# Attention scores on two 64-row halves, two tiles at a time, in a two-layer attention kernel

## What is computed

```python
xn = group_norm(x, 32 groups) * w + b                      # x: (8, 512, 1024)
qkv = einsum('oc,bct->bot', qkv_w, xn) + qkv_b             # 8 heads x (q, k, v) x 64 rows
weight = softmax(einsum('bct,bcs->bts', q, k) / 8)         # 1024 x 1024 for each head
a = einsum('bts,bcs->bct', weight, v)
x = x + einsum('oc,bct->bot', proj_w, a) + proj_b
```

## Time and profile before

| | us |
|---|---|
| median of 3 runs | 4324.97 |
| lowest and highest | 4324.69 and 4325.98 |
| the profiled execution, its own time | 4325.91 |
| its span, first to last instruction | 4323.8 |
| PE busy | 4282.4 |
| DVE busy | 3287.5 |
| ACT busy | 2918.6 |
| POOL busy | 2435.6 |

### The profile page before, as it was taken

How to read it: one execution, slowest core, us unless ns; L and a number is a source line. 1 busy time by engine, 2 the same in 40 slices (tenths; PEclk the granted TensorE clock), 3 DMA queues, 4 the chain that set the end, 5 groups by cost and what they waited for, 6 DMA issues and landing times.

```text
span 4323.8 us, 89926 instructions
## 1 busy us (share of the span) xinstructions
PE 4282.4 (99%) x26692; PEld 3739.6 (86%) x26692; DVE 3287.5 (76%) x5479; ACT 2918.6 (67%) x5375; POOL 2435.6 (56%) x2332
## 2 busy tenths in 40 slices
PE   8999999999999999999999999999999999999999
PEld 6888888888888888888888888888888888888888
DVE  5777867788686886877867778687886877868787
ACT  4757847577575775757757577575775757767576
POOL 5655556465564655646566465564655646556464
PEclk9999999999999999999999999999999999999999
DMA  3232222322223222232222222222222222222222
GB/s 87 49 96 47 71 72 49 96 47 78 65 49 96 47 80 65 47 95 49 78 74 58 87 47 82 64 65 80 47 79 67 66 79 48 80 64 68 75 49 88
DMA packets 99645, 295.08 MB, mean 68 GB/s; under 512 B 15104, under 2 KB 15232, under 8 KB 99328
## 3 DMA queue, kind: packets, MB, share of 16 engines
q1 hardware_dynamic: 99328, 291.19, 25.0%
HBM read 123.36 MB, written 33.55 MB: 36 GB/s over the span
## 4 chain that ended last, share of the span: by engine, by line
PE 94%; DVE 3%; POOL 2%; issue 1%; ACT 1%; DMA 0%; DVEq 0%; SPq 0%; POOLq 0%
PE ps_t L780 21%; PE ps_g L734 15%; PE ps_o L792 11%; PE ps_o L793 11%; PE ps_s L771 11%; PE ps_s L769 11%; PE ps_s L734 7%; PE ps_t L734 4%; PE ps_o L734 2%; POOL x_raw L382 2%; DVE xn_lo L644 1%; DVE rstd_bits L630 0%; DVE seed L628 0%; ACT xn_hi L491 0%; DVE pt_lo L587 0%
## 5 line engine op out<-in xcount | busy, mean ns | idle before, releaser
L376 POOL TENSOR_SCALAR probs<-probs,row_rcp 128x1024 f32<-128x1024 f32 x1024 | 1154.2, 1127 | 1365.8 <-DVE row_rcp L582 1365.8
L578 DVE TENSOR_REDUCE row_min<-ps_s 128x1 f32<-128x1024 f32 x1024 | 1250.6, 1221 | 213.4 <-PE ps_s L771 198.6
L480 ACT CAST pt_hi<-ps_t 128x512 fp32r<-128x512 f32 x2048 | 1112.6, 590 | 432.2 <-PE ps_t L780 421.7
L587 DVE TENSOR_TENSOR pt_lo<-ps_t,pt_hi 128x512 fp32r<-128x512 f32 x2048 | 1309.5, 680 | 9.5 <-ACT pt_hi L480 5.0
L475 ACT ACTIVATE probs<-ps_s,row_min 128x1024 f32<-128x1024 f32 x1024 | 1150.9, 1124 | 211.0 <-DVE row_min L578 194.2
L780 PEld LDWEIGHTS ps_t<-const_sb,probs 128*128 128x128 f32 x8192 | 945.1, 140 | 180.1 <-DVE pt_lo L587 50.3
L780 PE MATMUL ps_t<-const_sb,probs 128*128 128x128 f32 x8192 | 1084.4, 274 | 3.6 <-DVE pt_lo L587 3.4
L792 PE MATMUL ps_o<-pt_hi,v_st 128*128 128x256 f32 x4096 | 1044.1, 288 | 0.0
L793 PE MATMUL ps_o<-pt_lo,v_st 128*128 128x256 f32 x4096 | 1015.0, 282 | 0.0
L771 PE MATMUL ps_s<-kl_st,q_st 128*128 128x512 f32 x2048 | 808.5, 395 | 0.0
L769 PE MATMUL ps_s<-kh_st,q_st 128*128 128x512 f32 x2048 | 806.9, 394 | 0.0
(11 more groups left out here) (117 smaller groups left out, 4959.8 us busy)
## 6 DMA issues: line engine op xcount, KB each, us to landing
wqk_raw<-in_wqk SPq DMA_DIRECT2D x130, 256.0 KB, 2.6
q_st<-kh_st SPq DMA_DIRECT2D x128, 256.0 KB, 2.9
q_st<-kl_st SPq DMA_DIRECT2D x128, 256.0 KB, 3.6
kh_st<-kh_st SPq DMA_DIRECT2D x128, 256.0 KB, 2.9
kl_st<-kl_st SPq DMA_DIRECT2D x128, 256.0 KB, 3.6
x_raw<-layer_out SPq DMA_DIRECT2D x36, 512.0 KB, 5.4
wv_raw<-in_wv SPq DMA_DIRECT2D x66, 256.0 KB, 4.4
x_raw<-in_x SPq DMA_DIRECT2D x32, 512.0 KB, 5.5
```

Of the source, the lines that this page charges most:

```text
L376: nc.gpsimd.tensor_scalar(probs[m % 2][:, :], probs[m % 2][:, :], row_rcp[:, m % 4:m % 4 + 1], 1.0, ALU.mult, ALU.mult).then_inc(probs_rea ...
L480: nc.scalar.copy(pt_hi[:, m // 2 % 2, 4 * half:4 * half + 4, (m % 2) * P:(m % 2 + 1) * P], ps_t[:, half, :].rearrange("p (b t) -> p b t", ...
L578: nc.vector.tensor_reduce(row_min[:, m % 4:m % 4 + 1], ps_s[:, m % 2, :], AX.X, ALU.min).then_inc(min_ready, 1)
L587: nc.vector.tensor_tensor(pt_lo[place], ps_t[:, half, :].rearrange("p (b t) -> p b t", b=4), f32(pt_hi[place]), ALU.subtract).then_inc(lo_ ...
```

## The change

It does five things.

1. Scores: `stack` now keeps the split result straight (`hi_st`, `lo_st`: q in rows 0 to 63, k in rows 64 to 127) and builds a swapped copy (`hi_sw`, `lo_sw`: q in rows 64 to 127, and the first half of k's columns in rows 0 to 63). `scores` has six matmuls of 512 columns on 64 rows each: three on the top rows for the first 512 keys, three on the low rows for the second 512, alternately. They write different banks. The product of the two low parts is no longer formed.
2. Two tiles' scores stand one behind the other in every second step: in step m (even), tiles m + 2 and m + 3. The second waits for the exponential of tile m + 1. Tiles 0 and 1 of a pass and those of the last pair from tile 4 on are done singly.
3. The loops of all engines begin at step 2 of a pair and run into steps 0 and 1 of the next one; steps 0 and 1 of the first pair stand ahead of the loop, between the last two blocks of v. The last of a pair's eight weighted sums is made in steps 0 and 1 of the next pair (half in each) instead of whole behind step 15. Later q and k come as three matmuls in every step. The split of later q and k on POOL, and evacuations and copies on ACT, move by one or two steps.
4. DVE: a step's reciprocal for an odd tile stands in the following step, ahead of its row minimum. v's bias is added in `add_halves` instead of in `evac_v`.
5. Small memory moves: `wv_hi` and `wv_lo` use the other half of `pt_hi` and `pt_lo`; the row statistics share one tile, `row_stats`.

```diff
-LATER_QK_N = [3] * 12 + [2, 2, 2, 6]
+QK_PER_STEP = 3
-FILL_FROM = [1, 2, 3, 4, 6, 8, 10, 12, 14]
+FILL_FROM = [3, 4, 5, 6, 8, 9, 10, 12, 14]
...
             def stack(hd, s):
                 sp.wait_ge(qk_split, 2 * hd + 2)
-                sp.dma_start(f32(q_st[s][0:D, :]), f32(kh_st[s][0:D, :])).then_inc(q_moved, 16)
-                sp.dma_start(f32(q_st[s][D:P, :]), f32(kl_st[s][0:D, :])).then_inc(q_moved, 16)
-                sp.wait_ge(q_moved, 32 * (hd + 1))
-                sp.dma_start(f32(kh_st[s][0:D, :]), f32(kh_st[s][D:P, :])).then_inc(stacked[s], 16)
-                sp.dma_start(f32(kl_st[s][0:D, :]), f32(kl_st[s][D:P, :])).then_inc(stacked[s], 16)
+                for swapped, straight in ((hi_sw, hi_st), (lo_sw, lo_st)):
+                    sp.dma_start(f32(swapped[s][D:P, :]), f32(straight[s][0:D, :])).then_inc(stacked[s], 16)
+                    sp.dma_start(f32(swapped[s][0:D, 0:HALF]), f32(straight[s][D:P, 0:HALF])).then_inc(stacked[s], 16)
...
             def scores(m, s):
-                j = m % NT
-                for half in range(2):
-                    cols = slice(half * HALF, (half + 1) * HALF)
-                    nc.tensor.matmul(ps_s[:, m % 2, cols], q_st[s][:, j * P:(j + 1) * P], kh_st[s][:, cols],
-                                     start=True, stop=False)
-                    mm = nc.tensor.matmul(ps_s[:, m % 2, cols], q_st[s][:, j * P:(j + 1) * P], kl_st[s][:, cols],
-                                          start=False, stop=True)
+                tile = slice((m % NT) * P, (m % NT + 1) * P)
+                top, low = slice(0, D), slice(D, P)
+                first, second = slice(0, HALF), slice(HALF, T)
+                for n, (q, k) in enumerate(((0, 0), (1, 0), (0, 1))):
+                    nc.tensor.matmul(ps_s[:, m % 2, first], (hi_st, lo_st)[q][s][top, tile],
+                                     (hi_sw, lo_sw)[k][s][top, first], start=n == 0, stop=n == 2)
+                    mm = nc.tensor.matmul(ps_s[:, m % 2, second], (hi_sw, lo_sw)[q][s][low, tile],
+                                          (hi_st, lo_st)[k][s][low, second], start=n == 0, stop=n == 2)
                 mm.then_inc(scores_ready, 1)
...
+            def later_scores(i, p, m):
+                s = m // NT % 2
+                if m % NT == 0:
+                    pe.wait_ge(stacked[s], 64 * (4 * i + p + m // NT))
+                pe.wait_ge(exp_ready, TILES * i + PT_STEPS * p + m - 1)
+                scores(m, s)
...
+            def step(i, p, m):
+                if m % 2 == 0:
+                    later_scores(i, p, m + 2)
+                    later_scores(i, p, m + 3)
+                transpose(TILES * i + PT_STEPS * p + m, m)
...
+                step(i, 0, 0)
+                values(7)
+                step(i, 0, 1)
                 with pe.Fori(0, PAIRS - 1) as p:
-                    pair_steps(i, p, False)
-                    pair = PAIRS * i + p
-                    weigh(TILES * i + PT_STEPS * p, 8 * pair + 7, H * i + 2 * p + 1, 7, 0, BLK)
-                pair_steps(i, PAIRS - 1, True)
+                    for m in range(2, PT_STEPS):
+                        step(i, p, m)
+                        later_qk(i, p, m - 2)
+                        weigh_half(i, p, (m - 2) // 2, m % 2)
+                    for m in range(2):
+                        step(i, p + 1, m)
+                        later_qk(i, p, PT_STEPS - 2 + m)
+                        weigh_half(i, p, 7, m)
+                for m in range(2, PT_STEPS):
+                    last_step(i, m)
...
-                nc.vector.tensor_tensor(attn[rows, cols], ps_o[rows, 0:GROUP], o_part[k % 2][rows, :],
-                                        ALU.add).then_inc(attn_ready, 1)
+                nc.vector.scalar_tensor_tensor(out=attn[rows, cols], in0=ps_o[rows, 0:GROUP],
+                                               scalar=bv_sb[rows, bass.ds(lay * KT + p, 1)], in1=o_part[k % 2][rows, :],
+                                               op0=ALU.add, op1=ALU.add).then_inc(attn_ready, 1)
```

342 lines of the change are left out of this document (186 added, 156 removed).

## The result

| | us |
|---|---|
| before, median of 4 runs | 4324.83 |
| changed kernel, median of 4 runs | 4394.41 |
| lowest and highest | 4393.59 and 4396.38 |
| its profiled span | 4393.1 |

The changed kernel takes 1.0161 times the time of the kernel before, with a 95% interval of 1.0144 to 1.0179: it is **69.6 us slower**. The forecast was 4256 us, faster; the direction was wrong, and the time lies inside the range.

What follows compares the result with a forecast made beforehand. TensorE's own work was taken as the bound. 400 paired stretches gaining 0.195 us (78 us) and 224 single ones losing 0.04 us (9 us) gave -69 us, from 4325 to 4256 us; range 4120 to 4480 us.

Steps and rivals of the forecast that it cites:

- What bounds the kernel: Whole run: TensorE, busy 99% of the span, sets the time; shedding its instructions shortens the run if other engines keep up.
- Part 1: Scores: top-row and low-row matmuls stream together, so a tile takes three pitches, 0.70 us instead of 0.93, saving 0.23 us.
- Part 2: Ends of each half-row stretch: 0.11 us for the second stream's weight loads plus 0.08 us for each of two switches.
- the row that I took the price from: Trace of TensorE going from transposes to matmuls, 0.08 us, the only switch measured, used as the price per switch.
- The turning point: Switch price at which paired gains and single losses cancel: 400 x (0.355 - 2d) + 224 x (0.12 - 2d) = 0, d = 0.135 us.
- each switch empties the array: Rival at both ends of 624 stretches: 0.16 to 0.27 us a switch, 4356 to 4493 us; chance 30 in 100.
- Part 3: Moved bias, swap, copies, sums, splits and later q and k on the other engines and queues: booked at nothing.
- Part 4: Second tile of a paired stretch waits for the preceding tile's exponential: slack 0.34 or 0.26 us, so nothing booked.
- Under 10 us in all: Sign to look for: TensorE's total idle time at the second tile's scores, waiting for the exponential.
- a loss in it counts in full: Last pair, with 12 of the single stretches per pass: TensorE busy 34.00 of 34 us, so their loss counts wholly.

Runs made afterwards that it cites:

- e8: Changed kernel with two of the three low-row score matmuls left out of every tile, so part of the result is missing; 4418.39 us.
- e4: Kernel before, in its old order, with six 64-row score matmuls singly in each step, the new swap and v's bias in the addition; 4439.98 us.
- e1: Changed kernel with the last pair's copy and addition of halves put back at odd steps, as before the change; 4347.84 us.
- e11: Changed kernel with only SP's order altered: the last head's swap issued ahead of the next image's load; 4380.82 us.
- e12: e9 without the earlier split and evacuation of later q and k, that is e11 with the edits of e1 and e2; 4292.1 us.
- e7: Changed kernel with the edits of e1 and e2 and an earlier split and evacuation of later q and k, last pair's scores single; 4338.83 us.
- e9: e7 with the last head's swap issued on SP ahead of the next image's load; 4289.13 us.
- e2: Changed kernel with v's last block cut in two, half of it put behind the transposes of tile 1; 4371.8 us.
- e5: e1 with the last pair's scores paired too, two tiles at each even step; 4403.0 us.
- e10: e9 with the four 128-row score matmuls and the old swap of the kernel before; 4325.67 us.
- e3: Changed kernel, its order kept, with the four 128-row score matmuls and the old swap of the kernel before; 4512.93 us.

## Why the prediction was wrong

**What bounds the kernel: right before, no longer after.** TensorE's own work set the time, and an instruction taken off it would shorten the run, as long as the others keep up. That condition is what broke.

**Part 1, partners run side by side: right.** They start 0.01 us apart and six pairs take 6 x 0.23 us. e8 shows that the second stream costs at most 0.02 us in a stretch.

**Part 2, the ends: the term was too small.** Predicted 0.11 us for the second stream's loads and 2 x 0.08 for the switches, 0.27 us. Measured: no stagger of the second stream, since its weights come beside the first's (loads at 1046.53 and 1046.54 in the changed kernel); but 0.20 us going in and 0.16 us coming out, 0.36 us together by the timeline and 0.345 by e4. That is beyond the row that I took the price from, and 0.09 us per stretch more than predicted. The rule on tiling modes in the Trainium skill, page "TensorEngine Tiling (Array Packing)", section "Tiling Modes", that a change of mode drains TensorE, was the better guide than my row: the trace agrees in kind, with 0.20 and 0.16 us for the two changes, close to the lower price of an emptying (0.16 us). With it the sum is 400 x 0.11 = 44 us gained and 224 x 0.11 = 25 us lost, **-19 us where -69 us was predicted**. So this term was mis-sized by 50 us. It took most of the gain, but it didn't turn it into a loss.

The turning point was right as a formula: with 0.345 us for both ends, a paired stretch gains 0.465 - 0.345 = 0.12 us and a single one loses 0.11. By this alone the kernel would have been slightly faster. The rival "each switch empties the array", at 0.16 us a switch beside the 0.11 us, came out at 4356 us since it counted the load as well; the load was the part that isn't there.

**Part 3, edits at nothing: the step that failed.** That the copies and the sums stand one to two steps later and "their buffers are asked for a step or more after that" is false in the last pair. `ps_o` is asked for by the weighted sum right behind the transposes. In the loop later q and k cover the addition, and that cover is what I should have named; in the last pair it isn't there. e1 puts this at 46.6 us, and at 66.1 us once the swap is in time (e11 to e12). The swap on SP was booked at nothing by the earlier trace rows, where TensorE waits for none. That row told that it had arrived in time, not by how much. With later q and k spread evenly, the image's load moved from 13.2 to 8.3 us ahead of the swap's last part, and the two ran together. e11 puts it at 13.6 us, and once the other waits are gone e7 to e9 at 49.7 us.

**Part 4, the added wait: right where it was reckoned, missed where it wasn't.** In the loop it doesn't bind: past the loop's first stretch no score there waits for an exponential. At that first stretch, the head of the pass, where all of v's last block stands ahead of one tile's transposes and nothing behind, it costs 1.4 us a pass (e2, 22.6 us). In the last pair the change evades it with single scores, at 0.11 us each or more; e5 shows why. "Under 10 us in all" was 23.9.

**The account.** Loop over pairs: 400 paired stretches, -44 us. Single stretches: 224 x 0.112 = +25 us. The new order as such, by e10: up to -13 us. The waits: e9 takes them away and is 105.3 us below the changed kernel. Its parts are the additions 66.1, the head of the pass 22.6, the swap 13.6 and the earlier split 3.0 us. Sum +73 us; measured +69.6. By single differences from the changed kernel (e1, e2 and e11) the waits come to 46.6 + 22.6 + 13.6 = 83 us; the rest shows only when the swap is mended before the additions.

By place the same is seen. In the changed kernel the last pair from its step 2 to the projection takes 47.87 us of a pass (1046.54 to 1094.41), before 41.36 us (1036.64 to 1078.00), with one matmul of the projection fewer in it. Windows inside it, of the changed kernel, and in the loop, against the earlier trace rows:

```profile
600.00:700.00 100.00, 98.54 (x712) 83.74 (x712) 79.66 (x129) 75.47 (x142) 58.57 (x57) 1.00 0.16 40
1047.00:1088.00 41.00, 36.95 (x268) 28.74 (x265) 32.43 (x52) 28.35 (x56) 19.82 (x19) 1.00 0.39 116
```

In the loop TensorE is busy 98.5 of 100 us, 1.5 us short, with 15 stretches in it: about 0.1 us at the ends of each. In the last pair it is busy 36.95 of 41 us, where it had no gap in the earlier trace rows. I had read that stretch of before only for how full TensorE was, to say that a loss in it counts in full, and hadn't laid out its order after the change.

## What to carry to other kernels

When an order is changed for a loop, reckon each wait again at the loop's borders, the head and the last turn, where the filler that covers it in the loop is different or absent: here the loop gained 44 us and the waits at its borders cost over 100. "Nothing waits for it now" gives no slack; before a producer is moved later, read how long before its use it ended, and what shares its queue. And once several waits are on the path, taking one away enlarges another; only with all three gone (e9) did the change's own gain appear.

## What the runs showed of the hardware

Two matmuls on different 64-row halves start within 0.01 us of each other, their weight loads too, so a pair costs one pitch (0.23 us for 512 columns of 64 rows), and leaving out two of three low-row matmuls frees next to nothing (1.58 us against 1.60 for a stretch). Going from 128-row to 64-row matmuls cost 0.20 us and going back 0.16 us (e4: 0.345 us for both), while a tile saves 0.23 us: here half rows pay with two tiles in a stretch and not with one.

In the middle of the run, about a wait of 2.52 us, the granted clock fell from 2.4 to 1.2 GHz for 3.4 us (e7: pitch 0.42 instead of 0.23 us), so that this wait cost about 4.2 us. Such falls stand in the kernels whose swap was late (clock 0.997 in e1 and e7, 0.992 in e3), none in the middle of the changed kernel (longest wait there 2.0 us) or of e9. The length of the wait alone doesn't decide it: in e7 there was a fall behind 1.84 us and none behind 2.31 us, and in e8, where TensorE had fewer matmuls, eight behind 1.39 us.

The four DMAs of a swap, 128 and 256 KB, kept a score waiting until 8.7 us after the first was issued when they stood 6 us behind the 2 MB load of the next image, and no score waited for them when they were issued ahead of it (e9, e11).

A wait cost more than the idle time in the list: 0.61 us where the list has 0.39 (the sum at 1055.26 in the changed kernel), and 66.1 us by run times for 96 waits with 42.6 us in the list.
